# Records of five numbers in place of normalised rows: routing and expert stage of a graph layer with eight experts

## What is computed

```
xn  = layernorm(x)
x1  = x + gnn(xn, src, dst, edge_weight) + mix(xn)
z   = layernorm(layernorm(x1));  xn2 = z * gamma + beta
logits = xn2 @ Wr + br;  top 2 of 8;  w = softmax(top values)
for e in range(8):
    h = gelu(xn2 @ W1[e] + b1[e])
    y = y + (h @ W2[e] + b2[e]) * w_full[..., e, None]
out = x1 + y
```

## Time and profile before

| | us |
|---|---|
| median of the 3 runs shown | 4440.78 (4436.13 to 4442.04) |
| the profiled execution's own time | 4440.3 |
| its span, first to last instruction | 4438.6 |
| granted clock of TensorE over the span | 0.864 |

### The profile page before, as it was taken

How to read it: one execution, slowest core, us unless ns; L and a number is a source line. 1 busy time by engine, 2 the same in 40 slices (tenths; PEclk the granted TensorE clock), 3 DMA queues, 4 the chain that set the end, 5 groups by cost and what they waited for, 6 DMA issues and landing times. The chain is left out here.

```text
span 4438.6 us, 85552 instructions
## 1 busy us (share of the span) xinstructions
PE 3389.3 (76%) x16628; PEld 2802.7 (63%) x16629; DVE 2495.7 (56%) x11386; ACT 1685.6 (38%) x3095; POOL 3111.7 (70%) x2088
## 2 busy tenths in 40 slices
PE   1466666667677677878888888888758859999998
PEld 1355555555565555666666666666557758888887
DVE  3577777665555555666666666666548862222222
ACT  1233333344444443444444444444312224444443
POOL 0488888888888888888888888888855544444444
PEclk7788878788888888888888888888779979999999
DMA  9888888877777777777777777777789965565554
GB/s 380 241 146 155 152 148 147 157 117 118 116 109 115 116 113 114 102 108 108 105 104 107 108 103 105 108 107 102 91 217 296 294 187 143 139 145 141 141 140 114
DMA packets 588869, 638.95 MB, mean 144 GB/s; under 512 B 60524, under 2 KB 553156, under 8 KB 587138
## 3 DMA queue, kind: packets, MB, share of 16 engines
q0 software_dynamic: 279264, 269.84, 48.5%
q1 hardware_dynamic: 262234, 273.19, 20.9%
q10 hardware_dynamic: 47304, 95.18, 5.9%
HBM read 249.82 MB, written 390.09 MB: 144 GB/s over the span
## 5 line engine op out<-in xcount | busy, mean ns | idle before, releaser
L818 POOL DMA_INDIRECT agg<-msg,sidx x1664 | 2585.7, 1554 | 667.5 <-issue 408.7
L1122 PE MATMUL bank<-rows,Cmat 128*128 x3328 | 1025.7, 450 | 166.7 <-ACT msg L1315 140.6
L1315 ACT COPY msg<-bank 128x512 f32<-128x512 f32 x832 | 487.1, 585 | 1486.0 <-DMA agg<-msg,sidx 1209.8
L1122 PEld LDWEIGHTS bank<-rows,Cmat 128*128 128x128 f32 x3328 | 699.1, 224 | 346.7 <-issue 253.8
L873 DVE SCALAR_TENSOR_TENSOR sidx<-seen_sum,trash,srcf 128x4 int32<-128x4 f32 x416 | 92.7, 223 | 1022.8 <-DMA agg<-msg,sidx 1017.6
L2069 POOL DMA_INDIRECT out_dram<-x_y,x_node x210 | 325.7, 1551 | 473.1 <-issue 228.2
L856 DVE TENSOR_SCALAR Emat<-bank,srcf,wtf 128x128 f32<-128x128 f32 x1664 | 564.5, 398 | 0.0
L1106 PEld LDWEIGHTS bank<-Emat,pick 128*128 128x128 f32 x3328 | 518.3, 226 | 41.6 <-issue 17.7
L1106 PE MATMUL bank<-Emat,pick 128*128 128x128 f32 x3328 | 528.7, 311 | 1.6 <-DVE seen L860 1.6
L1097 PE MATMUL bank<-packed,both 128*128 (+1 forms) x416 | 187.3, 451 | 437.9 <-DVE seen L860 427.9
L860 DVE SCALAR_TENSOR_TENSOR seen<-bank,srcf,prior 128x128 f32<-128x128 f32 x1664 | 479.1, 341 | 0.0
(11 more groups left out here) (245 smaller groups left out, 4130.6 us busy)
## 6 DMA issues: line engine op xcount, KB each, us to landing
x_w<-in_L_ffn_W_dram SPq DMA_DIRECT2D x105, 512.0 KB, 4.1
agg<-expert_rows ACTq DMA_DIRECT2D x12, 4224.0 KB, 63.3
r_agg<-agg SPq DMA_DIRECT2D x196, 256.0 KB
x_zin<-table SPq DMA_DIRECT2D x105, 259.0 KB, 4.1
window_raw<-in_x_dram SPq DMA_DIRECT2D x208, 128.0 KB, 2.5
agg<-msg,sidx POOLq DMA_INDIRECT x1664
xn_rows<-n_xn ACTq DMA_DIRECT2D x49, 256.0 KB
xn_turned<-n_xnT ACTq DMA_DIRECT2D x49, 256.0 KB
```

What stands on the lines that cost most here:

```text
L818: pool.indirect_dma_start(scratch["agg"][r][:, :], bass.IndirectOffsetOnAxis(ap=sidx[:, j:j + 1], axis=0), msg[:, j % (2 * BATCH), :], Non ...
L1122: mm = nc.tensor.matmul(M[p][:, (q % 2) * D:(q % 2 + 1) * D], Cmat[:, b % 2, q, :], rows[:, bass.ds(slot, 1), :], start=True, stop=True)
L1315: nc.scalar.copy(msg[:, at:at + 2, :].rearrange("p q c -> p (q c)"), M[p][:, :]).then_inc(s_msg, 1)
```

## The change

- The table holds records of five numbers (`REC`): node, first choice, lead, mean and reciprocal deviation of x1. A record is 20 bytes where a row of `z` was 1036. Scatters, fills and table loads go by records. A fill record names node N, a row of x1 that belongs to no node.
- Routing writes no normalised row. x1 itself is turned (TensorE waits for `s_sum`), ScalarE copies it out in one instruction, and the router weights are changed once at the start so that the logits come out right: gamma is multiplied in, each column's mean over the features is taken off (`wrc`), beta's part goes to the bias (`brc`), and VectorE multiplies the product by the reciprocal deviation (two instructions in place of one). `normalise` becomes `scale`; the wait for the scatters moves ahead of the aggregation of the statistics.
- `add_halves` adds all four accumulators: the 128x1024 instruction, a wait, and one of 128x512. `sum_turned` turns one sum: four transposes in place of eight products.
- x1 is stored to `scratch["x1"]`, in place, and not to `out`. `out` is cleared in the edge stage: 25 writes by ScalarE from rows 28 to 31 of the zeros; SyncE waits for them ahead of `load_expert(7)`.
- In the expert stage records are loaded three blocks ahead (four slots, `SLOTS`, `AHEAD`), VectorE copies out the row numbers (`tell`), GpSimd gathers the 256 rows of x1 by two indirect DMAs (`gather`), three blocks ahead too and in program order ahead of the block's adds, and VectorE normalises the next block (`normalise`, two instructions of 128x256) into `zn`. The block of a row's first choice also adds x1 itself: `own` masks it, `xe` holds the masked rows, and the last instruction becomes weight times output plus `xe`. `over_blocks` unrolls four.

```diff
+REC = 5
+NODE, FIRST, LEAD, MEAN, RSTD = range(REC)
...
-        scratch = dict(scratch, table=scratch["table"][0])
+        scratch = dict(scratch, table=nc.dram_tensor("expert_records", (TABLE_ROWS, REC), F32, kind="Internal").ap())
...
+        BLANK = 4
+        blank = zeros[:, (CLEAR_ROWS - 1 - BLANK) * D:(CLEAR_ROWS - 1) * D]
...
+            sp.wait_ge(s_blankout, 16 * DOUBLES)
...
+            def blank_out(n):
+                if isinstance(n, int) and n == DOUBLES - 1:
+                    left = N - n * BLANK * P
+                    act.dma_start(out[N - left:N, :].rearrange("(p a) d -> p (a d)", a=2),
+                                  blank[0:left // 2, 0:2 * D]).then_inc(s_blankout, 16)
+                else:
+                    act.dma_start(out[bass.ds(n * BLANK * P, BLANK * P), :].rearrange("(p a) d -> p (a d)", a=BLANK),
+                                  blank).then_inc(s_blankout, 16)
...
+                steps = [(1, lambda u=u: deviations(n, u)) for u in pairs_of(n)] + [(8, lambda: blank_out(n))]
...
-                if last:
-                    sp.dma_start(out[(TILES - 2) * P:(TILES - 1) * P, :], x1[:, u % 2, 0]).then_inc(s_x1st[u % 2], 16)
-                    sp.dma_start(out[(TILES - 1) * P:N, :], x1[0:LAST, u % 2, 1]).then_inc(s_x1st[u % 2], 16)
-                else:
-                    sp.dma_start(pair_of(out, i), x1[:, u % 2]).then_inc(s_x1st[u % 2], 16)
+                sp.dma_start(pair_of(scratch["x1"], i), x1[:, u % 2]).then_inc(s_x1st[u % 2], 16)
...
-                                                z[:, u, c, :], None).then_inc(s_sent[c][m], 16)
+                                                rec[:, u, c, :], None).then_inc(s_sent[c][m], 16)
...
-            nc.gpsimd.memset(fill[:, :, D], float(NPAD)).then_inc(s_fill, 1)
+            nc.gpsimd.memset(fill[:, :, NODE], float(N)).then_inc(s_fill, 1)
...
+            for a in range(HALF):
+                nc.vector.tensor_scalar(wrg[:, a, :], wrt[:, a, :], gamma[:, a:a + 1], None, ALU.mult)
+                last = nc.vector.tensor_scalar(wrb[:, a, :], wrt[:, a, :], beta[:, a:a + 1], None, ALU.mult)
+            last.then_inc(s_wr, 1)
+            dve.wait_ge(s_wrs, 1)
+            dve.wait_ge(s_wr, 1)
+            for a in range(HALF):
+                nc.vector.scalar_tensor_tensor(out=wrc[:, a, :], in0=psum[2][:, 0:NE], scalar=-1.0 / D, in1=wrg[:, a, :],
+                                               op0=ALU.mult, op1=ALU.add)
+            nc.vector.tensor_tensor(brc[:], br[:], psum[2][:, NE:2 * NE], ALU.add).then_inc(s_wr, 1)
+            dve.wait_ge(s_wr, 2)
...
-                    dve.wait_ge(s_z, i - 1)
+                    dve.wait_ge(s_T, i - 1)
...
-                nc.vector.tensor_tensor(first_two, first_two, others, ALU.add).then_inc(s_half, 1)
+                nc.vector.tensor_tensor(first_two, first_two, others, ALU.add).then_inc(s_two, 1)
+                dve.wait_ge(s_two, i + 1)
+                one, other = [agg[:, u, 0, r].rearrange("p c d -> p (c d)") for r in range(2)]
+                nc.vector.tensor_tensor(one, one, other, ALU.add).then_inc(s_half, 1)
...
-            def normalise(i, u):
-                s = u % 2
-                dve.wait_ge(s_std, i + 1)
-                nc.vector.reciprocal(scl[:, s], std[:, s]).then_inc(s_scl, 1)
-                dve.wait_ge(s_scl, i + 1)
                 if not below(i, DEPTH):
...
-                nc.vector.tensor_copy(z[:, u, :, D], nodes[:, bass.ds(2 * i, 2)])
-                for c in range(2):
-                    last = nc.vector.tensor_scalar(z[:, u, c, 0:D], x1[:, s, c, :], mv[:, s, c, 0:1], scl[:, s, c:c + 1],
-                                                   ALU.subtract, ALU.mult)
-                last.then_inc(s_z, 1)
...
+                dve.nop(nofuse=True)
+                for c in range(2):
+                    last = nc.vector.bn_aggr(rec[:, u, c, MEAN:RSTD + 1], stat[:, c, :])
...
+            def scale(i, u):
+                s = u % 2
+                dve.wait_ge(s_std, i + 1)
+                nc.vector.reciprocal(rec[:, u, :, RSTD], std[:, s]).then_inc(s_scl, 1)
+                nc.vector.tensor_copy(rec[:, u, :, NODE], nodes[:, bass.ds(2 * i, 2)])
...
-                nc.vector.tensor_tensor(lg[:], logit, br[:].rearrange("p (a e) -> p a e", a=1).to_broadcast([P, 2, NE]),
-                                        ALU.add).then_inc(s_lg, 1)
+                dve.wait_ge(s_scl, i + 1)
+                for c in range(2):
+                    last = nc.vector.scalar_tensor_tensor(out=lg[:, c, :], in0=logit[:, c, :], scalar=rec[:, u, c, RSTD:RSTD + 1],
+                                                          in1=brc[:], op0=ALU.mult, op1=ALU.add)
...
-                        for r in range(NACC // 2):
-                            mm = nc.tensor.matmul(AT[u % 2][:, a * D + c * P:a * D + (c + 1) * P],
-                                                  agg[:, u, 0, r, c, a * P:(a + 1) * P], ident[:],
-                                                  start=(r == 0), stop=(r == NACC // 2 - 1))
+                        mm = nc.tensor.transpose(AT[u % 2][:, a * D + c * P:a * D + (c + 1) * P],
+                                                 agg[:, u, 0, 0, c, a * P:(a + 1) * P], ident[:])
...
-                pe.wait_ge(s_z, i + 1)
+                pe.wait_ge(s_sum, i + 1)
...
-                                                 z[:, u, c, a * P:(a + 1) * P], ident[:])
+                                                 x1[:, u % 2, c, a * P:(a + 1) * P], ident[:])
...
-                for a in range(HALF):
-                    last = nc.scalar.activation(xf[:, s, a, :], T[s][:, a * D:(a + 1) * D], ACT.Identity,
-                                                bias=beta[:, a:a + 1], scale=gamma[:, a:a + 1])
-                last.then_inc(s_xf, 1)
+                nc.scalar.copy(xf[:, s].rearrange("p a c -> p (a c)"), T[s][:, :]).then_inc(s_xf, 1)
...
+            def load_records(k, u):
+                at = sp.value_load(offset[0:1, bass.ds(SLOTS * k + u, 1)], min_val=0, max_val=TABLE_ROWS - CAP)
+                sp.dma_start(rec[:, u], scratch["table"][bass.ds(at, CAP), :].rearrange("(p a) d -> p a d", p=P)
+                             ).then_inc(s_rec[u], 16)
...
-                if not first(k):
-                    sp.wait_ge(s_T, q - 1)
-                    sp.nop(nofuse=True)
-                    sp.wait_ge(s_share, q - 1)
-                    sp.nop(nofuse=True)
-                sp.dma_start(zin[:, s], scratch["table"][bass.ds(at, CAP), :].rearrange("(a p) d -> p a d", p=P)).then_inc(s_z[s], 16)
-
+                if not over(q + AHEAD):
+                    if not below(q, 1):
+                        sp.wait_ge(s_share, q)
+                        sp.nop(nofuse=True)
+                    load_records(*ahead(k, u, AHEAD))
+
...
+                pe.wait_ge(s_zn, q + 1)
...
+            def tell(k, u):
+                dve.wait_ge(s_rec[u], 16 * k + 16)
+                nc.vector.tensor_copy(rows[:, u], rec[:, u, :, NODE]).then_inc(s_row, 1)
+
+            def normalise(k, u):
+                q, s = SLOTS * k + u, u % 2
+                dve.wait_ge(s_gat[u], 32 * k + 32)
+                if not below(q, 2):
+                    dve.wait_ge(s_T, q - 1)
+                for c in range(2):
+                    last = nc.vector.tensor_scalar(zn[:, s, c, :], xg[:, u, c, :], rec[:, u, c, MEAN:MEAN + 1],
+                                                   rec[:, u, c, RSTD:RSTD + 1], ALU.subtract, ALU.mult)
+                last.then_inc(s_zn, 1)
...
+                nc.vector.tensor_scalar(own[:, s], rec[:, u, :, FIRST], iota8[:, bass.ds(e, 1)], None, ALU.is_equal)
...
+                for c in range(2):
+                    last = nc.vector.tensor_scalar(xe[:, s, c, :], xg[:, u, c, :], own[:, s, c:c + 1], None, ALU.mult)
+                last.then_inc(s_xe, 1)
...
-                for c in range(2):
-                    nc.vector.tensor_scalar(y[:, s, c, :], y[:, s, c, :], share[:, s, c:c + 1], None,
-                                            ALU.mult).then_inc(s_y, 1)
+                dve.wait_ge(s_xe, q + 1)
+                for c in range(2):
+                    nc.vector.scalar_tensor_tensor(out=y[:, s, c, :], in0=y[:, s, c, :], scalar=share[:, s, c:c + 1],
+                                                   in1=xe[:, s, c, :], op0=ALU.mult, op1=ALU.add).then_inc(s_y, 1)
+
+            def body(k, u):
+                q = SLOTS * k + u
+                if not over(q + 1):
+                    normalise(*ahead(k, u, 1))
+                if not over(q + AHEAD):
+                    tell(*ahead(k, u, AHEAD))
+                shares(k, u)
+                finish(k, u)
+
+            for u in range(AHEAD):
+                tell(0, u)
+            normalise(0, 0)
             over_blocks(dve, body)
...
+            def gather(k, u):
+                pool.wait_ge(s_row, SLOTS * k + u + 1)
+                pool.nop(nofuse=True)
```

(11 more changed lines are left out.)

173 lines of the change are left out of this document (98 added, 75 removed).

## The result

The changed kernel takes 4532.0 us (median of 4 runs, 4525.8 to 4534.5) where the kernel before took 4439.6 us (4 runs beside it, 4436.1 to 4442.0). The ratio is 1.0207, 95% interval 1.0189 to 1.0224: slower by 92 us, where 19 us less were forecast. The profiled execution has a span of 4531.1 us.

What follows compares the result with a forecast made beforehand. GpSimd's issuing was taken to pace the edge stage, VectorE and DMA routing, TensorE the experts. Routing -19, fill -4, first block +4, experts 0 made -19 us: 4421 us from 4440.3, own bounds 4408 to 4431, range 4400 to 4452.

Steps and rivals of the forecast that it cites:

- The experts: 0 us: Expert stage: gathers and VectorE's added work hidden, the block staying at 7.35 us; 0 us.
- the DMA share stays near 0.57: Expert stage: the table's row load leaves, gathers move as much, so the DMA share stays near 0.57.
- Rival 2: Expert stage: GpSimd becomes the bound, with gathers from 1.2 us upwards; +5 to +74 us, middle 4458 us; 15%.
- the wait of L1655: Routing, VectorE: the 0.47 us per pair idle ahead of the first write into the 259 wide row were taken as gone.
- only moves, +0.08 us per pair: Routing, bound: if the wait at L1655 moves to another instruction, 0.08 us more per pair, +4 us.
- Routing, busy time: Routing, VectorE: 5.94 - 0.76 + 0.69 + 0.10 = 5.97 us busy per pair, the second add at 0.69 us.
- DMA in routing: Routing: 512 records at 12.5 ns, 0.4 us per pair; DMA 5.4 us of 6.72, share near 0.8.
- Rival 1: Routing: records cost the DMA engines what rows cost; routing gains 0 to 10 us, say 4437 us; 17%.
- the wait of L1655 only moves: Routing: another way to the time of rival 1, 4437 us, within its 17%.
- TensorE's clock: Routing: the clock may sink; with a fifth of the work at the lower level 5.3 us of 6.72, no bound.
- Fill and first block: Between routing and experts: fill -4 us (0 to -8), first block +4 us (2 to 8); the two cancel.
- The clears: Edge stage: 25 output writes of 512 KB taken as 0 us; 41 us if all stood in the way.

Runs made afterwards that it cites:

- a_w1two: Changed kernel with W1 loaded for the first two blocks alone, output wrong by that; 4432.4 us, 7.35 us a block.
- a_w1late: Changed kernel with the W1 load released by the end of the second product of block q-2 instead of the first; 4432.5 us.
- b_queue: Kernel before with a small table load that waits for the shares put ahead of each W1 load on SyncE's queue; 4575.9 us.
- a_swap: Changed kernel with the W1 load of block q+1 ahead of the record load of block q+3 on SyncE's queue; 4429.9 us, ratio 0.9986.
- b_gather: Kernel before plus two gathers of 128 rows a block into a spare tile, nothing waiting for them; 4434.5 us.
- a_both: Changed kernel with the edit of a_w1late and, in routing, the wait for scatters back at the scale; 4415.9 us, ratio 0.9956.
- b_sums: Kernel before with only the accumulators added in two VectorE instructions and one sum turned by four transposes; 4463.9 us, ratio 1.0062.
- b_w1mid: Kernel before with the z load ahead of W1 on SyncE's queue and W1 released by ScalarE's turned rows of block q-1; 4437.7 us.
- a_normahead: Changed kernel with rows normalised two blocks ahead instead of one, x_normal in four slots; 4427.3 us, 7.35 us a block.

## Why the prediction was wrong

**The step that failed** is "The experts: 0 us". Its sum had the length of GpSimd's chain right (1.85 + 4.76 + 0.95 us, no slack) and the price of what goes into the gap right (gathers at 1.00 us, hidden). But it took the landing, 4.76 us, as a constant. The landing is a term that depends on what else the DMA engines move at that moment: 3.7 us with no load beside it (a_w1two, a_w1late), 4.5 with the W1 load some 1.6 us ahead, 5.4 with it at the same time, 5.9 with the z load behind it as well (b_queue). The 4.76 us already held a load beside the first accumulate, where its 5.56 us cost nothing. The row loads were priced by their bytes, which stayed the same ("the DMA share stays near 0.57": it is 0.58), and not by their place. And the change of SyncE's program, records ahead of W1 and waiting for younger shares, was not weighed at all: of the moved loads I counted the bytes but not what is queued behind their wait. a_swap undoes this change of order alone and has 7.35 us a block; b_queue makes it alone in the kernel before and has 8.74. The 95 us are 105 blocks at 0.91 us.

**Rival 2** had the place (the chain of accumulates through GpSimd), the sign and nearly the upper end (+74 us), with a mechanism that is not there: gathers are not dearer than 1.2 us, and GpSimd is busy 64%, not above 85%. Its 15% were too few, for it was written as one price of one instruction, not as "a chain without slack gets longer by anything". The accumulate did get dearer, 1.65 us in place of 1.55. In a_w1two it takes 1.57 us with nothing of VectorE beside it and 1.66 us beside the masking of the residual and the small instructions ahead of it; the masking reads one tensor of rows and a mask of one number a row. In b_gather, with nothing of VectorE beside it, it takes 1.59. By itself this costs nothing, since a_w1two runs at 7.35 us a block. The Trainium skill (GPSIMD Engine Reference, Specifications) says that GpSimd contends with VectorE for SBUF on instructions with two SBUF inputs; the rows show a contention of 0.1 us, but no run here isolates the instructions with two.

**Routing, the wait of L1655.** "I take the 0.47 us as gone" failed. It was read too high to begin with: of the 19.8 us ahead of L1655 only 10.5, 0.25 us a pair, ended on the scatters, the rest on the reciprocal, which the change keeps. The wait for the scatters kept its count and moved 2.3 us up in VectorE's body, from behind the add of the accumulators to ahead of it. The time from positions through four scatters (1.3 us each on GpSimd) to their landing did not shrink with the bytes: a scatter lands 4.3 us after its start, 4.5 before. What the step gave as its bound, "only moves, +0.08 us per pair", is nearly what came: 27.4 / 41 = 0.67 us for 0.47, +0.2 us of waiting, and a pair of 7.2 us for 7.1 from the scatters. With the wait put back, a_both has 6.8 us where 6.72 were forecast; the rest of this sum was nearly right.

**Routing, busy time.** Right: 5.97 us foreseen, 6.0 found; second add 692 ns. b_sums has 0.56 us more a pair for it in the kernel before, and TensorE's shorter turns give nothing back. So this part of the change did not pay: it puts 0.69 us on VectorE, and the time a pair went up by most of that.

**DMA in routing.** Right: the share fell to 0.77, and the scatters took 1.8% of 16 engines in 300 us. That is 5280 packets at 16 ns, but 0.43 MB make 81 bytes a packet, some four records. A record thus cost 4 ns where 12.5 were taken, and a pair 0.13 us where 0.4 were. Rival 1's form with dear records is out; its other form, "the wait of L1655 only moves", is what happened in this stage.

**TensorE's clock** sank further than I had allowed, to 0.75 over the stage, where its busy share is 77% in place of 84%; b_sums shows it alone (0.72 in its window). It is not what keeps the pair at 7.2 us: a_both runs its pairs faster at 0.77. (My 5.3 us for a fifth of the work at the lower level should have been 5.1 by the two turns shown; nothing hangs on it.)

**Fill and first block** came to +1.2 us together, foreseen 0 with bounds that hold it. The terms of the first block add up to 8.9 us and not to the 8.6 written, which would have made +4.3 us of +4. **The clears** cost nothing: the first scatter stands at 3283 to 3291 us in all kernels with clears, and at 3288 to 3293 us in those without.

## What to carry to other kernels

A landing time read from a trace is no constant: it belongs to the loads that run beside it. Before moving a DMA to another place of a queue, write down for each DMA behind it what it now waits for, and ask whether a loop closes, from a landing through a wait to the issue of the load that delays that landing. Such a loop holds the load at a fixed distance behind the landing. That is harmless if the distance puts it beside a transfer that has slack (b_w1mid: beside the first accumulate, 7.37 us a block), and costs in every block if it puts it beside the transfer that lands last (the changed kernel, 8.31; b_queue, 8.74). In the kernel before, where the load follows TensorE instead, a collision with the second accumulate passed in a few blocks. And a wait moved up in an engine's program is not the same wait: it belongs just ahead of the instruction that needs it, at the price of a small copy if need be.

## What was not expected of the hardware

An accumulate of 128 rows of 1 KB lands 3.7 us after its issue began when no load is beside it (a_w1two), 5.4 us when a 512 KB load begins within 0.4 us of it (the changed kernel), and 5.9 us on average when a 259 KB load begins there as well (b_queue); two gathers issued right behind it change nothing (4.41 us in b_gather, 4.47 before). From the issue of the 5 KB record load to that of the W1 load behind it SyncE takes 1.22 or 1.58 us in the changed kernel, and 1.57 us from the small load to W1 in b_queue, where 0.7 us lie between W1 and z load in the kernel before; why was not settled. Why a_normahead's load comes to lie 2 to 4 us off the second accumulates, with SyncE's order unchanged, was not tested; its waits show VectorE waiting for gathered rows (205 us, 88 times) ahead of the shares, so that they no longer follow the landing.
